# Second cross attention of a decoder block: the window's edge made by selections on GpSimd instead of table products on TensorE, and a narrower last key block

## The reference

```
q = apply_rope(proj(query, Wq, bq)) * Dh ** (-0.5)
k = apply_rope(proj(key, Wk, bk))
v = proj(value, Wv, bv)
scores = jnp.einsum('bhqd,bhkd->bhqk', q, k)
rel = kv_idx - q_idx
mask = (rel > 0) | (rel < -WINDOW)          # WINDOW = 128
probs = jax.nn.softmax(jnp.where(mask, neg, scores), axis=-1)
out = einsum('bhqk,bhkd->bhqd', probs, v); return out @ Wo.T + bo
```

## Time and profile before

| what | value |
|---|---|
| median of 3 runs | 3013.92 us (3012.34 to 3017.2) |
| span of the profiled execution | 3008.1 us; the page gives no time of its own for it, so its time is this span and what the median has above it, 5.8 us |
| stage of the change, first cover to last exponential | about 2214 to 2629 us of the span |
| PE busy over the span | 92% |
| POOL busy over the span | 37% |

### The profile page before, as it was taken

One profiled execution on the slowest core, in us unless ns is written; L12 is line 12 of the kernel. 1 busy time (PEld: TensorE's weight loads), 2 busy tenths in 40 slices (PEclk: granted clock), 3 DMA queues, 4 the chain that ended last, 5 costly groups with the idle time before them and its releaser, 6 DMA issues. The chain is left out here.

```text
span 3008.1 us, 49289 instructions
## 1 busy us (share of the span) xinstructions
PE 2752.6 (92%) x16604; PEld 1616.4 (54%) x16605; DVE 1923.9 (64%) x3109; ACT 1450.5 (48%) x2231; POOL 1104.9 (37%) x853
## 2 busy tenths in 40 slices
PE   7997899999868899999999999999889999966998
PEld 4774333333335555555555555555445555556997
DVE  5775776667668766757575757575645555474565
ACT  3342566666668643434343434343335555553333
POOL 3233332222037243434343434443443333153333
PEclk9998899999989999999999999999989999958999
DMA  5002222222111000000000000000043222146665
GB/s 159 0 0 74 54 57 57 55 59 53 34 56 43 1 1 1 0 0 0 0 0 0 0 0 0 0 0 0 1 112 78 72 67 70 45 114 233 216 218 193
DMA packets 102929, 159.71 MB, mean 53 GB/s; under 512 B 28350, under 2 KB 63433, under 8 KB 97161
## 3 DMA queue, kind: packets, MB, share of 16 engines
q1 hardware_dynamic: 97784, 147.88, 17.1%
q0 software_dynamic: 3408, 8.46, 0.8%
q10 hardware_dynamic: 1600, 1.61, 0.2%
HBM read 91.79 MB, written 14.96 MB: 35 GB/s over the span
## 5 line engine op out<-in xcount | busy, mean ns | idle before, releaser
L1672 DVE TENSOR_REDUCE self_nmax<-self_SM 128x2 f32<-128x1024 f32 x256 | 313.9, 1226 | 184.5 <-PE self_SM L1569 177.7
L522 DVE TENSOR_REDUCE cross_nmax<-cross_S 128x2 f32<-128x1024 f32 x256 | 311.9, 1224 | 150.5 <-PE cross_S L347 149.6
L1650 ACT ACTIVATE self_PT<-self_ST 128x1024 f32<-128x1024 f32 x256 | 262.6, 1026 | 292.0 <-PE self_ST L1592 292.0
L1710 POOL TENSOR_TENSOR self_U<-self_PT 128x1024 f32<-128x1024 f32 x64 | 153.0, 2391 | 622.1 <-ACT self_PT L1650 622.1
L1713 POOL TENSOR_TENSOR self_U<-self_U,self_PT 128x1024 f32<-128x1024 f32 x128 | 304.0, 2375 | 55.6 <-ACT self_PT L1650 51.1
L456 ACT ACTIVATE cross_PT<-cross_S 128x1024 f32<-128x1024 f32 x256 | 260.9, 1026 | 114.6 <-PE cross_S L358 113.9
L1186 DVE TENSOR_REDUCE cross_nmax<-cross_S 128x4 f32<-128x1024 f32 x128 | 156.8, 1225 | 143.4 <-PE cross_S L984 143.3
L1602 PE MATMUL self_OP<-self_PT,self_V 128*64 128x512 f32 x1024 | 233.8, 598 | 10.1 <-ACT self_PT L1650 10.1
L1686 DVE RECIPROCAL self_rcp<-self_W 128x512 f32<-128x512 f32 x64 | 214.1, 3345 | 8.4 <-PE self_W L1609 8.4
L1112 ACT ACTIVATE cross_PT<-cross_S 128x1024 f32<-128x1024 f32 x128 | 131.1, 1024 | 119.6 <-PE cross_S L1000 119.6
L1602 PEld LDWEIGHTS self_OP<-self_PT,self_V 128*64 128x64 f32 x1024 | 69.5, 136 | 139.2 <-issue 132.8
(11 more groups left out here) (436 smaller groups left out, 6335.7 us busy)
## 6 DMA issues: line engine op xcount, KB each, us to landing
moe_staged<-in_L_ffn_W SPq DMA_DIRECT2D x36, 1024.0 KB
cross_ks<-cross_parts SPq DMA_DIRECT2D x384, 64.0 KB, 2.2
cross_qs<-cross_parts SPq DMA_DIRECT2D x376, 64.0 KB, 2.3
all_x<-in_L_ffn_W SPq DMA_DIRECT2D x14, 1024.0 KB
all_x<-sorted_rows SPq DMA_DIRECT2D x83, 130.0 KB, 2.3
cross_cT<-in_ctx_T SPq DMA_DIRECT2D x16, 512.0 KB, 4.5
sorted_rows<-all_spare_row SPq DMA_DIRECT2D x1, 5460.0 KB, 23.8
all_x<-in_x SPq DMA_DIRECT2D x8, 512.0 KB, 3.7
```

The source lines that it names most:

```text
L522: dve.tensor_reduce(nmax[:, g % 2, 0:R, n % PER_G], S[:, slot[st], :, :], AX.X, ALU.max, negate=True).then_inc(s_maxed, 1)
L1650: act.activation(PT[:, k, :, :], ST[:, :, :], ACT.Exp).then_inc(exped.sem, 1)
L1672: dve.tensor_reduce(nmax[:, i, 0:P:D], SM[:, :, :], AX.X, ALU.max, negate=True).then_inc(maxed.sem, 1)
L1710: pool.tensor_tensor(U[:, c % 2, :, :], PT[:, 0, :, :], PT[:, 1, :, :], ALU.add).then_inc(added.sem, 1)
```

## The change

- The covers of `exact` are gone. Covers remain for `max` only, so the table has three columns of blocks instead of four.
- `exact` is now first in a unit, due at u; then the cover of max(u+8), then max(u+8). `exact` itself waits for the slot.
- The second key block of a t = 1 unit is 128 queries wide instead of 256, and the exponential of such a unit covers 384 columns of each head, not 512.
- A new step `band` on POOL, due at u + 0.5: two `affine_select` in place on the exponentials of a unit, the first over the four blocks of 128 x 128 on the diagonal (512 columns), the second over the blocks one further (512 columns for t = 0, 256 for t = 1). They put a zero where a condition on partition number and column fails. `value` waits for both of the unit (`s_banded`) instead of the exponential.
- The third operation of `rope`, with its waits, becomes a step `low` of its own, 2.6 units later in POOL's list.
- With `exact` at whole units, where times are equal the exponential now comes ahead of `htok` and `high` in ACT's list.

```diff
             at[("high", b, n)] = o + t + 5.0
+            at[("low", b, n)] = o + t + 5.6
         at[("bias", b, 0)] = o - 8.0
...
         for u in range(UNITS):
-            at[("cover_exact", b, u)] = o + u
-            at[("cover_max", b, u)] = o + u - LEAD + 0.02
-            at[("exact", b, u)] = o + u + 0.04
+            at[("band", b, u)] = o + u + 0.5
+            at[("cover", b, u)] = o + u - LEAD + 0.02
+            at[("exact", b, u)] = o + u
             at[("max", b, u)] = o + u - LEAD + 0.06
...
              ("rot", 0, 3): -28.2, ("rope", 0, 3): -28.0, ("high", 0, 3): -27.8,
+             ("low", 0, 1): -29.1, ("low", 0, 3): -27.75, ("low", 0, 2): -26.4,
              ("rot", 0, 2): -27.7, ("rope", 0, 2): -27.5, ("high", 0, 2): -26.5, ("cast", 0, 0): -28.9, ("bias", 0, 0): 2.0}
...
     ACT_DMA = [("stack", 0, 0, 3), ("mdma", 0, 0)]
-    COVERS = ("cover_max", "cover_exact")
-    pe_steps = in_order(RINGED + COVERS + ("max", "exact", "value"))
+    pe_steps = in_order(RINGED + ("cover", "max", "exact", "value"))
     nth_full = counted(finishing([st for st in pe_steps if st[0] in RINGED]))
...
     for n, st in enumerate(pe_steps):
-        if st[0] in COVERS + ("max", "exact"):
+        if st[0] in ("cover", "max", "exact"):
             continue
...
     for st in pe_steps:
-        if st[0] in COVERS:
-            st = (st[0][6:],) + st[1:]
+        if st[0] in ("cover", "exact"):
+            st = ("max",) + st[1:] if st[0] == "cover" else st
             slot[st] = len(seen) % SLOTS
...
     nth_turn = counted([st for st in dve_steps if st[0] == "turn"])
-    pool_steps = in_order(("root", "rope", "bias"))
+    pool_steps = in_order(("root", "rope", "low", "band", "bias"))
     pool_steps.remove(("rope", 0, 0))
+    pool_steps.remove(("low", 0, 0))
     nth_rope = counted([st for st in pool_steps if st[0] == "rope"])
...
         bvs, bo = s.sb("bvs", [P, KC, P]), s.sb("bo", [P, C])
-        band = s.sb("band", [P, 2, 4, 2 * P], BF16)
-        band32 = PT[:, 0:2, :, :].rearrange("p h r (i c) -> p h (r i) c", i=2)
+        band = s.sb("band", [P, 2, 3, 2 * P], BF16)
+        band32 = PT[:, 0:2, :, :].rearrange("p h r (i c) -> p h (r i) c", i=2)[:, :, 0:3, :]
         S = s.ps("S", [P, SLOTS, R, 512])
...
         s_load, s_set, s_pad, s_ones, s_init = s.sem("load"), s.sem("set"), s.sem("pad"), s.sem("ones"), s.sem("init")
+        s_banded = s.sem("banded")
         s_early, s_wv, s_stack_act, s_mrow_act = (s.sem(n) for n in ("early", "wv_in", "stack_act", "mrow_act"))
...
                 kind, b, n = st[:3]
-                if kind in COVERS:
-                    t = unit(n)[1] + (kind == "cover_exact")
-                    if st == ("cover_max", 0, 0):
+                if kind == "cover":
+                    t = unit(n)[1]
+                    if b == 0 and n == 0:
                         pe.wait_ge(s_cast, 1)
-                    dst = free_slot((kind[6:], b, n))
+                    dst = free_slot(("max", b, n))
                     for r in range(R):
...
                         rows_in(pe, b, g)
-                    dst = S[:, slot[st], :, :]
+                    dst = free_slot(st)
                     for i in range(2):
                         k0 = (2 * t + i) * P
-                        q0 = min(k0, T - 2 * P)
+                        qn = min(2 * P, T - k0)
                         for r in range(R):
                             rows_r = slice(HALF * r, HALF * r + MROWS)
-                            m = pe.matmul(dst[:, r, 2 * P * i:2 * P * (i + 1)], ks[rows_r, p, k0:k0 + P], qs[rows_r, p, q0:q0 + 2 * P],
-                                          start=False, stop=(i == 1), skip_group_check=True)
+                            m = pe.matmul(dst[:, r, 2 * P * i:2 * P * i + qn], ks[rows_r, p, k0:k0 + P], qs[rows_r, p, k0:k0 + qn],
+                                          start=True, stop=True, skip_group_check=True)
                     m.then_inc(s_scored, 1)
...
                         pe.wait_ge(s_act, nth_act[("v", b, k // 2, 1)])
-                    pe.wait_ge(s_exped, nth_exact[("exact", b, PER_G * g + k // 2 * 2 + 1)])
+                    pe.wait_ge(s_banded, 2 * nth_exact[("exact", b, PER_G * g + k // 2 * 2 + 1)])
                     q0, qn = k * P, min(2 * P, T - k * P)
-                    from_ = 2 * P * (k % 2) + 2 * P - qn
+                    from_ = 2 * P * (k % 2)
                     for j in range(4):
...
                         act.wait_ge(s_cast, 1)
-                    act.activation(PT[:, pt_slot[st], :, :], S[:, slot[st], :, :], ACT.Exp).then_inc(s_exped, 1)
+                    act.activation(PT[:, pt_slot[st], :, 0:T - P * unit(n)[1]], S[:, slot[st], :, 0:T - P * unit(n)[1]], ACT.Exp).then_inc(s_exped, 1)
                 elif kind == "value":
...
             pool.wait_ge(s_set, 3)
+            zero = pool.to_reg(0.0)
             for st in pool_steps:
...
                     pool.tensor_tensor(xt, xt, bo[:, :].unsqueeze(1).to_broadcast([P, NT, C]), ALU.add).then_inc(s_bias, 1)
-                else:
+                elif kind == "band":
+                    t = unit(n)[1]
+                    probs = PT[:, pt_slot[("exact", b, n)], :, :].rearrange("p r c -> p (r c)")
+                    upto = probs.rearrange("p (j x) -> p j x", x=2 * P)[:, :, 0:P]
+                    since = probs.rearrange("p (j x) -> p j x", x=2 * P * (1 + t))[:, :, P:2 * P]
+                    pool.wait_ge(s_exped, nth_exact[("exact", b, n)])
+                    pool.affine_select(upto, upto, [[0, 2 * R], [1, P]], ALU.is_ge, zero, base=0, channel_multiplier=-1).then_inc(s_banded, 1)
+                    pool.affine_select(since, since, [[0, 2 * R // (1 + t)], [-1, P]], ALU.is_ge, zero, base=0, channel_multiplier=1).then_inc(s_banded, 1)
+                elif kind == "rope":
                     row, base = rows[:, n % 2, :], ROPE * (nth_rope[st] - 1)
...
                     pool.tensor_tensor(row, turned, rsin[:, n % 2, :], ALU.add).then_inc(s_rope, 1)
-                    pool.wait_ge(s_rope, base + 2)
+                else:
+                    row = rows[:, n % 2, :]
+                    pool.wait_ge(s_rope, ROPE * (nth_rope[("rope", b, n)] - 1) + 2)
                     pool.wait_ge(s_high, nth_high[("high", b, n)])
...
         both = np.where((other >= mine) & (other <= mine + P), 0.0, NEG)
-        halves.append(np.stack([np.where(other <= mine, 0.0, NEG), both, both, np.where(other >= mine + P, 0.0, NEG)], 1))
+        halves.append(np.stack([np.where(other <= mine, 0.0, NEG), both, both], 1))
     c["window_band"] = np.stack(halves, 1).astype(f)
```

## The result

The changed kernel takes 3009.34 us (median of 12 runs, 3005.34 to 3016.99) against 3013.79 us of the kernel before (12 runs): a ratio of 0.9981 with a 95% interval of 0.9974 to 0.9989, by which it is 5.7 us less (3.3 to 7.8); the medians themselves lie 4.5 us apart. I had forecast no change, 3014.8 us. The time lies in my range of 3002 to 3034 us, but the interval leaves out 1.0, and the gain goes the way of my first rival. On another chip the same kernel gave 0.9989 (0.9975 to 1.0002), which does not exclude no change.

A forecast was written before the change was run, and what follows sets the result against it. PE was taken to bound the stage, others waiting for it. Terms -1.1 + 6.5 - 2.6 - 1.9 = +0.9 us on the 3008.1 us span, plus 5.8 us to the median, gave 3014.8 us; range 3002 to 3034.

The forecast's parts named there:

- my first rival: The narrow key block saves time with its columns: 3005.1 us in all, -8.8 us; chance 0.26.
- the narrower key block: Score products of 128 columns in t = 1 units take two passes: +0.12 us each, +6.5 us over 54.
- Covers and order: PE's unit of exact, cover, max takes 1.20 us instead of 1.22, +0.01 for new neighbours: -1.1 us over 109 units.
- Short units: Eleven units waiting for DVE: the max slot's circle falls from 2.40 to 2.16 us, -2.6 us in all.
- Last eight units: Units without max: four covers fewer each, four narrow blocks, +0.3 for waiting on selections; together -1.9 us.
- Selections: POOL's selections take 0.67 us each, giving 37.9 us of work in a 52.55 us batch entry; hidden, costing nothing.
- The moved step: In POOL's list, rope starts after selections and low comes about 2 us later, with 5.6 us in hand: no cost.

The follow-up runs named there:

- wide_last: The changed kernel with the last key block 256 queries wide again: ratio 0.9999 to the kernel before, 52.22 us a batch entry.
- same_again: The changed kernel once more without an edit, on another chip: ratio 0.9989 to the kernel before, 51.77 us a batch entry.
- before: The kernel before the change, unedited, in its first profile: 52.55 us a batch entry, 454.3 us for the stage.
- before_again: The kernel before the change, unedited, profiled once more: 52.55 us a batch entry, 452.1 us for the stage.
- narrow_alone: The kernel before with the 128-query key block as its only edit: 52.51 us a batch entry, against 52.55 without it.

## Why the prediction was wrong

The step that failed is **the narrower key block**, the +6.5 us of the sum. I bound it by -2.7 and +6.5 us over 54 blocks and took the upper end, "the row nearest in width, tile count and operand bytes". It measured -0.056 us each in the steady stretch, -3.0 us over 54: the lower end, and one record for each product, not two. What misled me was a row of another operand type, chosen for its shape: the value products' two passes come with their type, for those of 256 columns show two passes as well (96 records for 48 instructions). That row spoke for type and against width, and it stood in my own list. (By that row a pass is 0.13 us, so even my upper end should have been +0.14 us and not +0.12.)

With the measured price, in the 54 blocks and in the four of the last units, my sum gives -1.1 - 3.0 - 2.6 - 2.6 = -9.3 us instead of +0.9. The whole time fell by 5.7 us (3.3 to 7.8), the stage by 5.5 to 9.3 us in the profiles. So the corrected sum is at the far end of the stage and too large for the whole. Part of the rest goes with the clock, for which the sum had no term: it fell to 0.50 once before the end of the stage in each profile of the changed kernel and in neither profile of the kernel before. The two profiles of the changed kernel, one with the fall and one without, differ by 0.8 us in the short units (41.84 and 41.00) and by 2.7 between exponentials 119 and 127 (16.04 and 13.31).

The other terms:
- *Covers and order*: -0.02 + 0.01 us a unit forecast, -0.021 measured (1.35 us over 63 units, from wide_last). Right, and the +0.01 for the new neighbour was not needed: exact follows each kind of product at the same distance as the covers did (0.20, 0.31 or 0.52 us by kind, in both kernels).
- *Short units*: 2.16 us instead of 2.40 forecast, and measured. Two reductions of the changed kernel, where a round in the earlier trace rows took 2.40 us:

```profile
2606.53 1.23 DVE L1189 TENSOR_REDUCE cross_nmax<-cross_S 128x4 f32<-128x1024 f32 x1 [0.40 <-PE cross_S L987]
2608.69 1.23 DVE L1189 TENSOR_REDUCE cross_nmax<-cross_S 128x4 f32<-128x1024 f32 x1 [0.94 <-PE cross_S L987]
```

But only eight of the rounds there were of 2.40 us; those of 2.51 stayed at 2.50. So the piece gave -2.1 at full clock and -1.3 at 0.96, where -2.6 over eleven units was forecast. DVE was still what is late there: in the changed kernel's profile no value product of the short units waited for POOL.
- *Last eight units*: -1.9 us forecast, -2.6 with the measured narrow block; the last piece gave -1.1 in one profile and +1.7 in the other. The clock makes the difference: 0.50 from 2610 to 2616 in the first profile of the changed kernel, 1.00 in the second over the same units. At full clock it is -1.8 us between exponentials 119 and 127 (15.08 to 13.31) and +0.7 behind the last one, where +0.3 was forecast for the wait for selections.
- *Start*: up to exponential 40 the profiles gained 1.7 to 4.0 us, of which 40 units x 0.05 are 2.0. The two profiles of the kernel before differ by 2.1 us there, so the rest can't be told from chance.
- *Selections*: 0.67 us each forecast, 0.64 measured; POOL 37.9 us a batch entry forecast, 36.95 measured. POOL became the bound somewhere between 88% of the batch entry (nothing) and 99% (1.7 us a batch entry); I had put the point at 100%. The Trainium skill's 12 cycles per element for branching (GPSIMD Engine Reference, Elementwise — side-by-side cycle accounting) is not what a selection does: 0.64 us is an eighth of what it gives. The compare-and-select figures of the Trainium skill (GPSIMD Engine Reference, Performance pitfalls for Q7 kernels), an estimated 0.44 to 0.87 us, hold the measured time.
- *The moved step*: I put rope and low at nothing with the move, which nothing contradicts: PE is busy all of a batch entry in the changed kernel. What the selections would cost without the move, 200 us, I had not priced.

## What to carry to other kernels

Count changes between unlike products on TensorE as well as products: here four products fewer were worth 0.21 us a unit with like ones side by side, and 0.02 with one change more. In this kernel a narrower product saved its columns only where no like product followed at once. Where work goes to an engine with an ordered queue, look first for that queue's own waits for others: one wait ahead of the new work cost 200 us, while filling the engine to 88% cost a steady batch entry nothing. And when a row stands in for one that is missing, look first whether another row of the same type already separates type from shape.

## What the runs showed of the hardware

- A product of 128 columns whose operands the code declares fp32r runs in one pass (16 records for 16 products), and a pair of them holds TensorE 0.06 us less than a pair of 256 (0.37 us against 0.43 for the group).
- In a row of like products with 128-column weights, the loads of a pair start 0.11 to 0.12 us apart whatever the columns of the products, and a pair of 128 columns pushed the next pair from 0.12 to 0.17 us.
- One change more between unlike products cost 0.20 us a unit: the same three groups take 1.21 us in one order and 1.01 in another with a change less.
- A selection of 128x512 in fp32 takes 0.64 us on GpSimd, one of 128x256 0.41; in a row those of 512 start 0.59 us apart.
- The granted clock fell from 1.00 to 0.50, from 2.4 to 1.2 GHz, over 2610 to 2616 us, after PE had been busy 4.03 of 5.00 us in front of DVE's reductions; the kernel before was busy 4.14 of 5 us in the like stretch and kept 1.00; same_again had 0.96 over its short units and 1.00 behind them. Over the last two pieces the three profiles with the covers of exact (before, before_again, narrow_alone) kept 1.00 throughout, and each of the eleven without them fell to 0.50 at least once. That goes with the shorter PE program in stretches that another engine paces; what decides each fall is not shown.
